# GpSimd takes over the weighing of one channel half in a state-space scan, with the engines' orders written anew

## What is computed

```
# block 1: selective scan, 16 states per channel
u = causal_conv(layernorm(x)); dt, B, C = split(u @ xproj)
delta = softplus(dt @ dtproj + bias)
h[t] = exp(delta[t]*A) * h[t-1] + delta[t]*u[t]*B[t]     # for each channel and state
y[t] = sum over the 16 states of h[t]*C[t];  x += y + u*D
# block 2: per-batch expert with int8-like rounding: gate/up, silu, down
x += quant_linear(silu(gate)*up, w_out[b]),  gate, up = quant_linear(layernorm(x), w_in[b])
# block 3: feed-forward, 704 wide, same rounding
x += quant(silu(gate)*up) @ quant(w_down).T,  gate, up = quant(layernorm(x)) @ quant(w_gate_up).T
```

## Time and profile before

| what | us |
|---|---|
| median of 3 runs | 250.27 (250.07 to 250.71) |
| the profiled execution | 251.69 |
| its span, first to last instruction | 249.9 |
| DVE busy | 220.4 (88%) |
| PE busy | 168.8 (68%) |
| ACT busy | 144.7 (58%) |
| POOL busy | 144.6 (58%) |
| mean granted TensorE clock | 0.888 of full |

### The profile page before, as it was taken

How to read it: one execution, slowest core, us unless ns; L and a number is a source line. 1 busy time by engine, 2 the same in 40 slices (tenths; PEclk the granted TensorE clock), 3 DMA queues, 4 the chain that set the end, 5 groups by cost and what they waited for, 6 DMA issues and landing times.

```text
span 249.9 us, 2858 instructions
## 1 busy us (share of the span) xinstructions
PE 168.8 (68%) x676; PEld 98.6 (39%) x676; DVE 220.4 (88%) x419; ACT 144.7 (58%) x307; POOL 144.6 (58%) x174
## 2 busy tenths in 40 slices
PE   0187498898485497867577479649878768729434
PEld 0155364464141344443423335234545446415232
DVE  2759989999999989989999999989899997894861
ACT  4018537965859375675566787346456886535151
POOL 3540898485456499457599564761484827551442
PEclk9999689999959769799999999776999997975957
DMA  6985643365353234352354644000000000000003
GB/s 179 341 298 104 230 135 109 110 138 116 84 127 113 98 114 138 127 129 77 90 155 148 152 98 129 0 0 0 1 3 1 21 0 0 25 0 0 0 0 126
DMA packets 15103, 23.23 MB, mean 93 GB/s; under 512 B 1136, under 2 KB 6640, under 8 KB 15088
## 3 DMA queue, kind: packets, MB, share of 16 engines
q1 hardware_dynamic: 13792, 21.92, 30.7%
q10 hardware_dynamic: 1296, 1.15, 1.4%
HBM read 21.88 MB, written 1.18 MB: 92 GB/s over the span
## 4 chain that ended last, share of the span: by engine, by line
DVE 35%; issue 22%; PE 19%; ACT 7%; POOL 7%; DMA 5%; SPq 2%; POOLq 0%; DVEq 0%; ACTq 0%
DVE Q L1043 8%; PE pY L741 6%; DVE prod L1054 6%; DMA fs_t<-w_in_t 5%; PE Q L229 3%; DVE am L980 3%; PE Q L893 3%; PE pA L708 2%; DVE w L1212 2%; POOL drive L354 2%; DVE tf L1219 2%; POOL w L384 2%; PE pX L229 2%; PE pA L229 1%; ACT Q L498 1%
## 5 line engine op out<-in xcount | busy, mean ns | idle before, releaser
L354 POOL TENSOR_TENSOR drive<-du,bc 128x512 f32<-128x512 f32 x64 | 79.9, 1272 | 31.2 <-DVE Q L1043 27.0
L741 PE MATMUL pY<-prod,ident 128*128 128x512 f32 x128 | 69.1, 678 | 12.7 <-DVE prod L1054 7.5
L1043 DVE TENSOR_TENSOR_SCAN Q<-Q,drive 128x512 f32<-128x512 f32 x64 | 75.1, 1212 | 0.8 <-ACT Q L498 0.8
L498 ACT ACTIVATE Q<-delta,negA 128x255 f32<-128x255 f32 x128 | 54.8, 470 | 24.9 <-DVE Q L1043 24.4
L1054 DVE TENSOR_TENSOR prod<-Q,bc 128x512 f32<-128x512 f32 x64 | 41.2, 674 | 0.9 <-PE pY L741 0.9
L741 PEld LDWEIGHTS pY<-prod,ident 128*128 128x128 f32 x128 | 25.5, 215 | 41.0 <-issue 27.9
L384 POOL TENSOR_TENSOR w<-w 128x352 f32<-128x352 f32 x16 | 15.4, 974 | 12.4 <-DVE w L1212 12.3
L229 PE MATMUL Q<-ident,w 128*128 128x128 f32 x48 | 10.1, 374 | 14.0 <-ACT w L597 14.0
L301 POOL TENSOR_SCALAR ve<-mv 128x2 f32<-128x2 f32 x12 | 3.9, 325 | 25.0 <-DVE mv L971 24.9
L1212 DVE TENSOR_TENSOR w<-Q,ws 128x704 f32<-128x704 f32 x16 | 13.6, 880 | 0.8 <-PE Q L877 0.5
L229 PEld LDWEIGHTS Q<-ident,w 128*128 128x128 f32 x48 | 7.6, 191 | 16.1 <-ACT w L597 15.8
(11 more groups left out here) (154 smaller groups left out, 330.3 us busy)
## 6 DMA issues: line engine op xcount, KB each, us to landing
bc<-bc_dram SPq DMA_DIRECT2D x32, 512.0 KB, 4.8
w<-w_gate_up SPq DMA_DIRECT2D x1, 1408.0 KB, 9.6
x_sb<-x SPq DMA_DIRECT2D x4, 256.0 KB, 3.6
fs_t<-w_in_t SPq DMA_DIRECT2D x1, 1024.0 KB, 12.4
out<-x_sb ACTq DMA_DIRECT2D x8, 128.0 KB, 1.8
w<-w_down SPq DMA_DIRECT2D x1, 704.0 KB, 11.0
ctx_t<-w_out_t SPq DMA_DIRECT2D x1, 512.0 KB, 12.7
xproj<-xproj_t SPq DMA_DIRECT2D x1, 160.0 KB, 3.0
```

What stands on the lines that cost most here:

```text
L354: pool.tensor_tensor(drive[:, s % 2, h], du[:, b, h].unsqueeze(1).to_broadcast([P, SPS, T]), bc[:, g % 4, 0].rearrange("p (n t) -> p n t", ...
L498: act.activation(decay[:, h, n, 1:T], delta[:, b, h, 1:T], ACT.Exp, scale=negA[:, h, k:k + 1]).then_inc(S["decay_ready"], 1)
L741: ins = pe.matmul(pY[:], ident[:], prod[:, s % 2, :, n, :], start=(s == 0 and n == 0), stop=False, skip_group_check=True)
L1043: dve.tensor_tensor_scan(hid[:, h].rearrange("p n t -> p (n t)"), decay[:, h].rearrange("p n t -> p (n t)"), drive[:, s % 2, h].rearrange( ...
```

## The change

The weighing of half 1 goes from DVE to POOL. POOL doesn't read PSUM, so the scan of half 1 writes its states to a new SBUF tile with two buffers, `hid_sb`; that of half 0 keeps one PSUM bank (`hid` = bank 2; bank 3 is no longer used in the stage). The semaphore `weighed` is split in `weighed0` (DVE) and `weighed1` (POOL). The scan of half 0 now waits for the weigh of the step just before it, that of half 1 for POOL's weigh of two steps before. All four lists of calls are written anew.

```diff
+        hid_sb = sb("hid_sb", [P, 2, SPS * T])
-        hid = Q[:, 2:4].rearrange("p h (n t) -> p h n t", n=SPS)
+        hid = Q[:, 2]
 # SP, before the load of bc for step g
-                    sp.wait_ge(S["weighed"], H * (g - 3))
+                    sp.wait_ge(S["weighed0"], g - 3)
+                    sp.wait_ge(S["weighed1"], g - 3)
 # POOL
+            def weigh(b, s):
+                g = STEPS * b + s
+                pool.wait_ge(S["scanned"], H * g + 2)
+                if g >= 2:
+                    pool.wait_ge(S["summed"], g - 1)
+                pool.tensor_tensor(prod[:, s % 2, 1].rearrange("p n t -> p (n t)"), hid_sb[:, s % 2], bc[:, g % 4, 1], ALU.mult)\
+                    .then_inc(S["weighed1"], 1)
...
+            drive_step(0, 0, 1); drive_step(0, 1, 0); drive_step(0, 1, 1); drive_step(0, 2, 0); weigh(0, 0)
+            drive_step(0, 2, 1); weigh(0, 1); drive_step(0, 3, 0); drive_step(0, 3, 1); drive_step(0, 4, 0)
...
+            drive_step(1, 3, 0); weigh(1, 1); drive_step(1, 3, 1); drive_step(1, 4, 0); neg_mean(1, 0)
+            drive_step(1, 4, 1); var_eps(1, 0); prep_du(2); rsqrt(1, 0); weigh(1, 2); prep_du(3); norm2(0)
+            weigh(1, 3); drive_step(1, 5, 0); drive_step(1, 5, 1); smooth1(0); weigh(1, 4); floor1(0)
...
+            drive_step(3, 4, 0); drive_step(3, 4, 1); var_eps(1, 2); weigh(3, 2); rsqrt(1, 2); smooth2(1)
+            drive_step(3, 5, 0); neg_mean(1, 2); weigh(3, 3); floor2(1); residual2(0); drive_step(3, 5, 1)
...
+            neg_mean(2, 0); rsqrt(2, 0); weigh(3, 5); norm3(0); smooth1(2); weigh(3, 6); floor1(2)
+            drive_step(3, 7, 1); residual2(1); weigh(3, 7); var_eps(2, 1); rsqrt(2, 1); gated3(0, 0, 0)
 # PE sum_step
-                pe.wait_ge(S["weighed"], H * (g + 1))
+                pe.wait_ge(S["weighed0"], g + 1)
+                pe.wait_ge(S["weighed1"], g + 1)
 # PE turn_q3(0) and mm3(0, 0, c), which write the banks of the scan
-                    pe.wait_ge(S["weighed"], H * NB * STEPS)
+                    pe.wait_ge(S["weighed0"], NB * STEPS)
+                    pe.wait_ge(S["scanned"], H * NB * STEPS)
 # DVE
             def scan(b, s, h):
...
-                if u >= 2:
-                    dve.wait_ge(S["weighed"], u - 1)
-                dve.tensor_tensor_scan(hid[:, h].rearrange("p n t -> p (n t)"),
+                if h == 0 and g >= 1:
+                    dve.wait_ge(S["weighed0"], g)
+                if h == 1 and g >= 2:
+                    dve.wait_ge(S["weighed1"], g - 1)
+                dve.tensor_tensor_scan(hid_sb[:, s % 2] if h else hid,
...
-            def weigh(b, s, h):
+            def weigh(b, s):
...
+            scale_w12(); round_w1(1); wmax_in(2); scan(0, 0, 0); weigh(0, 0); scan(0, 0, 1); scan(0, 1, 0)
...
+            weigh(0, 4); scan(0, 5, 0); weigh(0, 5); round_w1(3); scan(0, 5, 1); scan(0, 6, 0); scan(0, 6, 1)
+            wmax_in(3); round_w1(5); round_w1(7); wmax_ctx(0); round_w1(9); weigh(0, 6); scan(0, 7, 0)
+            scan(0, 7, 1); weigh(0, 7); scan(1, 0, 0); scan(1, 0, 1); prep_bc(3); weigh(1, 0); scan(1, 1, 0)
+            wmax_ctx(1); prep_relu(2); prep_relu(3); scan(1, 1, 1); weigh(1, 1); scan(1, 2, 0); scan(1, 2, 1)
+            round_w2(0); residual1(0); stats2(0); prep_delta(2); weigh(1, 2); scan(1, 3, 0); prep_delta(3)
+            wmax_inv(); norm2(0); weigh(1, 3); scan(1, 3, 1); scan(1, 4, 0); weigh(1, 4); scan(1, 4, 1); amax_x(0)
...
+            scan(3, 2, 1); gate_up1(1); gate1(1); up1(1); max_ad(0); scale_ad(0); inv_ad(0); residual1(2)
+            amax_a(1); stats2(2); weigh(3, 2); scan(3, 3, 0); ratio_a(1); scan(3, 3, 1); norm2(2); weigh(3, 3)
+            scan(3, 4, 0); expert_out(0); scan(3, 4, 1); inv_smooth2(1); weigh(3, 4); scan(3, 5, 0); weigh(3, 5)
...
+            amax_x(2); ratio_x(2); norm3(0); scan(3, 7, 0); max3(0); scale3(0); inv3(0); quant3(0); expert_out(1)
+            inv_smooth1(2); weigh(3, 7); scan(3, 7, 1); stats3(1); max_w(2); scale_w1(2); inv_w1(2); max_x(2)
 # PE list, start
-            prep_turn(0); prep_bc(0); prep_dt(0); prep_turn(1); prep_pre(0); prep_conv(1); prep_bc(1)
+            prep_turn(0); prep_dt(0); prep_turn(1); prep_bc(0); prep_pre(0); prep_conv(1); prep_bc(1)
...
```

More of the change, by code:

```diff
@@ L396, in _ @@
[L396 to L401, removed]
@@ L407, in _ @@
[L407 to L412, removed]
@@ L413, in _ @@
[L413 to L417, removed]
@@ L1305, in _ @@
-            scan(0, 7, 0); scan(0, 7, 1); weigh(0, 7, 0); weigh(0, 7, 1); prep_relu(2); scan(1, 0, 0)
-            scan(1, 0, 1); wmax_ctx(1); weigh(1, 0, 0); round_w1(5); round_w1(7); round_w1(9); prep_relu(3)
-            weigh(1, 0, 1); scan(1, 1, 0); scan(1, 1, 1); weigh(1, 1, 0); wmax_inv(); weigh(1, 1, 1); prep_bc(3)
-            scan(1, 2, 0); scan(1, 2, 1); residual1(0); weigh(1, 2, 0); stats2(0); weigh(1, 2, 1); scan(1, 3, 0)
-            scan(1, 3, 1); weigh(1, 3, 0); weigh(1, 3, 1); round_w2(0); scan(1, 4, 0); norm2(0); scan(1, 4, 1)
@@ L1315, in _ @@
-            scan(2, 2, 0); scan(2, 2, 1); residual1(1); weigh(2, 2, 0); stats2(1); weigh(2, 2, 1); gate1(0)
-            scan(2, 3, 0); scan(2, 3, 1); weigh(2, 3, 0); weigh(2, 3, 1); up1(0); norm2(1); scan(2, 4, 0)
-            amax_a(0); scan(2, 4, 1); amax_x(1); weigh(2, 4, 0); weigh(2, 4, 1); ratio_x(1); ratio_a(0)
-            prep_delta(3); scan(2, 5, 0); scan(2, 5, 1); weigh(2, 5, 0); weigh(2, 5, 1); scan(2, 6, 0)
-            scan(2, 6, 1); inv_smooth1(1); weigh(2, 6, 0); weigh(2, 6, 1); scan(2, 7, 0); scan(2, 7, 1)
@@ L1330, in _ @@
-            expert_out(1); gate_up3(0, 0, 0); gate_up3(0, 0, 1); stats3(1); gate_up3(0, 1, 0); gate_up3(0, 1, 1)
-            open3(0, 0); max4(0, 0); open3(0, 1); scale4(0, 0); max4(0, 1); inv4(0, 0); scale4(0, 1)
-            factor4(0, 0); inv4(0, 1); norm3(1); factor4(0, 1); max3(1); gate_up1(2); residual1(3); scale3(1)
-            stats2(3); inv3(1); quant3(1); down(0, 0); gate1(2); norm2(3); up1(2); amax_a(2); ratio_a(2)
-            down(0, 1); amax_x(3); ratio_x(3); inv_smooth2(2); gate_up3(1, 0, 0); gate_up3(1, 0, 1)
@@ new lines, in _ @@
+            max_x(0); scale_x1(0); round_w2(1); inv_x1(0); weigh(1, 6); scan(1, 7, 0); scan(1, 7, 1); max_w(0)
+            scale_w1(0); inv_w1(0); weigh(1, 7); scan(2, 0, 0); weigh(2, 0); scan(2, 0, 1); scan(2, 1, 0)
+            scan(2, 1, 1); weigh(2, 1); scan(2, 2, 0); scan(2, 2, 1); weigh(2, 2); scan(2, 3, 0); scan(2, 3, 1)
+            weigh(2, 3); residual1(1); stats2(1); scan(2, 4, 0); scan(2, 4, 1); weigh(2, 4); scan(2, 5, 0)
+            norm2(1); gate_up1(0); gate1(0); up1(0); scan(2, 5, 1); amax_a(0); weigh(2, 5); ratio_a(0); amax_x(1)
@@ new lines, in _ @@
+            gate_up3(0, 1, 1); open3(0, 0); max4(0, 0); open3(0, 1); scale4(0, 0); max4(0, 1); inv4(0, 0)
+            scale4(0, 1); factor4(0, 0); max3(1); inv4(0, 1); factor4(0, 1); gate_up1(2); scale3(1); residual1(3)
+            stats2(3); inv3(1); quant3(1); gate1(2); down(0, 0); norm2(3); up1(2); amax_a(2); ratio_a(2)
+            down(0, 1); amax_x(3); ratio_x(3); inv_smooth2(2); gate_up3(1, 0, 0); gate_up3(1, 0, 1); max_ad(2)
+            inv_smooth1(3); scale_ad(2); gate_up3(1, 1, 0); inv_ad(2); gate_up3(1, 1, 1); open3(1, 0); max_x(3)
@@ new lines, in _ @@
+            max_w(3); scale_x1(3); max4(1, 0); scale_w1(3); inv_x1(3); inv_w1(3); open3(1, 1); expert_out(2)
+            scale4(1, 0); max4(1, 1); inv4(1, 0); scale4(1, 1); factor4(1, 0); inv4(1, 1); factor4(1, 1)
+            stats3(2); gate_up1(3); gate1(3); up1(3); norm3(2); amax_a(3); ratio_a(3); max3(2); scale3(2); inv3(2)
+            down(1, 0); inv_smooth2(3); quant3(2); down(1, 1); max_ad(3); scale_ad(3); inv_ad(3)
+            gate_up3(2, 0, 0); gate_up3(2, 0, 1); gate_up3(2, 1, 0); open3(2, 0); gate_up3(2, 1, 1); max4(2, 0)
```

210 lines of the change are left out of this document (102 added, 108 removed).

## The result

The changed kernel takes 254.03 us (252.61 to 254.81) against 250.17 (250.06 to 250.71) for the kernel before, run beside it: a ratio of 1.0154, interval 1.0106 to 1.0202. Forecast were 247.6 us. The profiled execution of the changed kernel took 254.22 us with a span of 251.9; the one of before lay 1.4 us above its median (rows 1 are of that execution), so the two spans differ by 2.0 us where the medians differ by 3.9.

A forecast was written before the change was run, and what follows sets the result against it. DVE was taken to bound the scan stage before, POOL after (133 us against 125). Minus 1.0 us in the stage and minus 1.7 in the tail made minus 2.7, from 250.27 to 247.6 us; range 242 to 254.5.

The forecast's parts named there:

- POOL is the new bound of the stage: Scan stage: POOL needs 133 us against DVE's 125, so only 9.4 of DVE's 16 us are left, before any wait.
- wrong at the root: Sign against the forecast: DVE is still full in the scan stage.
- The price on POOL: Scan stage: each of 32 new products costs a drive's 1.24 us, bounds 1.0 and 1.5; POOL needs 133 us together.
- DVE then needs about 125 us for the stage: Scan stage: DVE's work falls from 140.7 to about 122 us without 32 weighs, plus 3 us of lost overlap.
- I take 3: DVE in the scan stage: lost overlap between dependent weighs and scans, up to 0.08 us a time, at most 5 us.
- The sum is 8.4 us: POOL's waits in the scan stage, bounds 3 and 15 us, putting the last scan at 171.1 us, 1.0 us sooner.
- The walk: Stepping through POOL's and DVE's lists with the forecast durations to find where POOL waits; 8.4 us in all.
- The start, kept: Start of the stage: POOL's drive of (0,1,0) still begins at 29.56 us, bounds 28 and 31.5.
- The tail, -1.7: After the last scan: a weigh and `expert_out(1)` leave DVE's tail, saving 1.7 us, bound 2 us either way.
- B: Rival, scan stage: DVE and POOL block each other, 22 us on DVE and 7 on POOL; 254.5 us, chance 0.25.
- C: Rival, scan stage: PE's sum delays DVE's weighs, 2 to 3 us in all, nothing won; 250.3 us, chance 0.15.
- A: Rival, scan stage: POOL stays fed, its waits are 3 us instead of 8.4; 242.2 us, chance 0.20.

The follow-up runs named there:

- e4: The changed kernel with logarithm outputs of batches 1 and 3 and tanh outputs of batches 0 and 1 in the free PSUM bank; 254.69 us, ratio 1.0200.
- e6: The changed kernel with the order of work ahead of the first scan as in the kernel before; 259.2 us, ratio 1.0398.
- e1: The changed kernel's lists, but both halves weighed on DVE, each from its own PSUM bank; 262.96 us, ratio 1.0539.
- e3: The changed kernel with the lists of before, POOL weighing half 1 behind the first drive two steps later; 261.40 us, ratio 1.0506.
- e8: The lists of the kernel before, with POOL weighing half 1 in even steps only and DVE in odd ones; 254.77 us, ratio 1.0221.
- e8b: As e8, with each POOL weigh one drive later in POOL's list; 269.21 us, ratio 1.0828.

## Why the prediction was wrong

**Which engine bounds the stage:** right for the kernel before, wrong for the changed one. POOL's waits on scans fell from 27 us to 6.9 (1.7 and 5.2 in the groups), and POOL is at 91% of the stage. But "POOL is the new bound of the stage" asked for idle time of DVE before scans, released by drives, and no gap above 0.15 us is; DVE is still full, which the prediction had named as being wrong at the root.

**The price on POOL, 1.24 us in its queue, 133 us in all:** right. From the drive of (0,1,0) at about 29.5 to the end of the last drive at 176.36 POOL is busy for 133.2 us:

```profile
29.50:176.36 146.86, 106.89 (x353) 57.24 (x351) 138.84 (x198) 93.52 (x215) 133.24 (x125) 0.90 0.40 104
```

**"DVE then needs about 125 us for the stage":** this is the step that failed. It was busy for 137.2. The missing 12 are 8.6 us of stretched instructions, for which the sum had nothing, 1.8 of other work and scans (0.9 is `expert_out(1)`, which came in from the tail, and 0.65 a maximum, `wmax_in`), 1.2 for two weighs too many in the sum, and 0.8 of overlap. For the two weighs: of the kernel before's 64, two lie behind its last scan, so 30 went and not 32; the sum of the tail counts these two again. For the overlap: of the 6.2 us in the table 2.4 are the overlap of the 30 removed weighs themselves, 0.08 each, which 0.59 had allowed for; 3.8 stand against "I take 3". The bound of 0.08 us a time was wrong, though, as it came from instructions without a wait between them: where a scan follows that needs the weigh's result at once, it is 0.21, 0.13 of it idle time.

**"The sum is 8.4 us" of waits on POOL:** measured 146.9 - 133.2 = 13.6 (the bound was 15). The walk let DVE catch up with 10 us to spare; with DVE at 137 there was no such slack, and the places of the walk came out longer: the one in batch 3 is 2.10 us where 1.5 stood, because its block lasts 6.2 and not 4.4. Of these 1.8 us, 1.4 are `gate1` and `up1` stretched, and most of the rest a scaling and a reciprocal behind the maximum that the walk had left out. The longer waits are 5.2 us and carry the last scan from the forecast 171.1 to 176.6 nearly alone. That DVE's growth causes them is read from the trace, where 11.7 of the 13.6 us end with an instruction on DVE; no run shows it, as e4 took 3.4 us of DVE's work away and the stage stayed within 0.4 us.

**The start, kept:** POOL's began as forecast; DVE's first scan came 3.6 us later, which I hadn't costed. As POOL runs ahead by two or three half steps only, it came to wait for DVE there. Half of the 3.6 is stretching again. In e6, the one try to take it back, the time grew.

**The tail, -1.7:** measured -2.5, within its bound.

Together: +5.2 of waits, some 0.3 of rounding in the stage, -0.8 in the tail: +4.7 on the forecast of -2.7 makes the +2.0 of the spans. The forecast had the sign wrong; that the range of 242 to 254.5 still holds 254.03 is owed to B's end of it alone.

**The rivals.** B, "Slower: DVE and POOL shut each other out", gave 254.5 us, and 254.03 were measured; its mechanism is shown by the durations (1370 ns against 424 in e4), its working only in half. It had 22 us of stretching on DVE, 18 more than before; measured are 8.6 more, 0.25 for each of 35 instructions. And it had 7 us on POOL; the drives went from 1272 to 1289 ns, 1.1 us for 64 of them, though seven took over 1320 ns, up to 1582. That the number was met is luck: 5.2 us more of waits on POOL, which B kept at 8.4, stood in for the rest. The Trainium skill, "SBUF — State Buffer", section "Who interferes with whom", tells it as a lock that holds either side for the other's whole instruction. In these traces DVE's side pays (a 13-column scaling took 1.31 us) and POOL's hardly (the 17 ns above). The section also says that a VectorE instruction with at most one SBUF input, outside the two-port modes, doesn't contend; e4 agrees (424 ns). I gave B 0.25 because the trace of before showed only 4 us of stretching at 67% of POOL; that was itself a share of the work on the bounding engine, and more of POOL's work had to raise it. C, PE's sum in the way: DVE waited 1.3 us for pY in all, so it was small. A, POOL fed: its 3 us of waits were 13.6.

## What to carry to other kernels

Taking work from the full engine to a neighbour is worth its time in the queue, less what the neighbour does to the instructions that stay: look in the trace of before for durations of one shape that vary (343 and 969 ns), count how many such instructions stay, and price them at the new load. A second engine at over 90% isn't by that the new bound: here POOL was busy for 91% of the stage, and DVE, at 95%, waited 0.7 us for it. See how long before its reader each result is done, and sum the waits with both engines' new durations; here a relief of one engine alone brought nothing clear of noise. And handwritten lists are tied to a split: with the lists of the other split, e1 and e3 took 12 to 13 us more than the kernel before.

## What the runs showed that was not expected

- A scan on DVE that waits for the weigh right before it starts 0.21 us later than one that doesn't (0.79 against 0.58 from the weigh's start); put into the kernel before, where it strikes in 13 places, it cost 4.3 us (2.1 to 6.5), 2.8 of stage in the profile.
- SBUF-only operations on DVE took up to 1.37 us instead of 0.42 beside POOL's products, small ones too: 13 columns took 1.31 us. The same operations with one operand in PSUM never did, nor did reductions and statistics from SBUF.
- A scan that writes to SBUF took 1204 ns, one that writes to PSUM 1225.
- Moving each of POOL's 16 products one drive later in the list (e8 to e8b) cost 14 us.
